# A transposed copy of x1 by DMA instead of TensorE, o_rec in PSUM, and a new order on GpSimd and VectorE

## What is computed

```python
# 1. causal attention over x with one more key and value made from cond (16 heads of 16)
q, k, v = split(x @ c_attn_w + c_attn_b); k = concat(k_img, k); v = concat(v_img, v)
a = softmax(where(causal, q @ k.T / 4, -10000) + mask) @ v @ c_proj_w + c_proj_b
# 2. linear attention over a, a residual and a layer norm
q2, k2, v2 = relu(a @ Wq.T + bq), relu(a @ Wk.T + bk), a @ Wv.T + bv
y = (q2 @ (k2.T @ v2)) / max(q2 @ sum(k2), 1e-6) + a
x1 = x + layernorm(y) * gamma + beta
# 3. an LSTM over the 64 rows of each sequence as time steps (batch 64), then an FP4 FFN
for t in range(64): gates = x1[:, t] @ Wx + h @ Wh + b; c, h = cell(gates, c)
out = x1 + (silu(fp4(h) @ fp4(w_gate).T) * (fp4(h) @ fp4(w_up).T)) quantized again @ fp4(w_down).T
```

## Time and profile before

| | us |
|---|---|
| median of 3 runs | 1044.33 |
| lowest, highest | 1040.74, 1045.4 |
| profiled execution | 1042.76 |
| its span, first to last instruction | 1040.8 |
| busy in the span: TensorE, VectorE, ACT, GpSimd | 892.0, 885.0, 500.4, 343.1 |
| mean granted clock of TensorE | 0.95 of full speed |

### The profile page before, as it was taken

The page is one execution under the profiler, slowest core; times in us unless marked ns, Lnnn a source line. Parts: engine busy times, 40 slices in busy tenths (PEclk is TensorE's granted clock), DMA queues, the critical chain, the costliest instruction groups (busy, mean ns, idle before and its releaser), DMA issues. The chain is left out here.

```text
span 1040.8 us, 27556 instructions
## 1 busy us (share of the span) xinstructions
PE 892.0 (86%) x9862; PEld 595.3 (57%) x9862; DVE 885.0 (85%) x2157; ACT 500.4 (48%) x1177; POOL 343.1 (33%) x436
## 2 busy tenths in 40 slices
PE   3477887988888888888987799999999999999984
PEld 2255555666666666666655456656565566656553
DVE  5489889799999999999985488888888888888884
ACT  2356446466667666766664333334433333434431
POOL 0126446455555555555563011111111111111111
PEclk9589789799999999999998999999999999999997
DMA  4500000101110111011100000000000000000001
GB/s 109 190 13 22 27 19 18 35 19 34 33 33 17 33 33 33 18 32 33 34 22 16 11 7 16 22 21 21 21 21 21 21 17 16 20 21 21 21 21 26
DMA packets 37143, 30.37 MB, mean 29 GB/s; under 512 B 12081, under 2 KB 35953, under 8 KB 37076
## 3 DMA queue, kind: packets, MB, share of 16 engines
q1 hardware_dynamic: 37076, 29.42, 10.0%
HBM read 20.87 MB, written 8.54 MB: 28 GB/s over the span
## 5 line engine op out<-in xcount | busy, mean ns | idle before, releaser
L663 POOL TENSOR_TENSOR ffn_room<-h_value,h_scale 128x704 f32<-128x704 f32 x32 | 44.3, 1386 | 292.7 <-DVE h_value L171 292.7
L711 PE MATMUL bank<-gu,xqT 128*128 128x512 f16 (+1 forms) x576 | 130.1, 366 | 0.7 <-DVE xqT L1542 0.7
L886 PE MATMUL bank<-wh,h 128*64 128x512 f16 x768 | 100.3, 385 | 3.5 <-ACT h L1157 2.1
L875 PE MATMUL bank<-wx,x1T 128*64 128x512 f16 x768 | 93.7, 379 | 0.9 <-DVE x1T L440 0.9
L611 POOL TENSOR_TENSOR p<-prob,p 128x520 f16<-128x520 f32 x64 | 79.1, 1236 | 43.6 <-ACT p L1065 43.6
L987 PE MATMUL bank<-dn,hqT 128*128 128x256 f16 x576 | 70.7, 279 | 19.6 <-DVE hqT L1527 19.6
L1147 ACT ACTIVATE sig<-bank 128x256 f32<-128x256 f32 x64 | 24.6, 385 | 127.3 <-PE bank L886 126.7
L875 PEld LDWEIGHTS bank<-wx,x1T 128*64 128x64 f16 x768 | 78.6, 201 | 11.4 <-DVE x1T L440 1.2
L711 PEld LDWEIGHTS bank<-gu,xqT 128*128 128x128 f16 x576 | 54.2, 99 | 53.9 <-issue 11.3
L776 PE MATMUL bank<-ident,p 128*65 128x128 f16 x1024 | 78.8, 228 | 1.4 <-POOL p L611 0.8
L604 POOL TENSOR_TENSOR prob<-prob,row_max 128x520 f32<-128x520 f32 x64 | 68.2, 1066 | 31.0 <-DVE row_max L1325 31.0
(11 more groups left out here) (201 smaller groups left out, 2192.2 us busy)
## 6 DMA issues: line engine op xcount, KB each, us to landing
x_in<-in_x SPq DMA_DIRECT2D x32, 128.0 KB, 2.2
x_res<-in_x SPq DMA_DIRECT2D x32, 128.0 KB, 2.1
x_rows<-x_rows_sb SPq DMA_DIRECT2D x32, 128.0 KB
ffn_room<-x_rows SPq DMA_DIRECT2D x64, 64.0 KB, 2.2
out<-ffn_room SPq DMA_DIRECT2D x64, 64.0 KB, 2.0
mask_in<-in_mask_Bx1x1xS_ff SPq DMA_DIRECT2D x64, 16.0 KB, 2.4
x1T<-in_L_cond_Wx SPq DMA_DIRECT2D x1, 1024.0 KB, 6.2
x1T<-in_L_cond_Wh SPq DMA_DIRECT2D x1, 1024.0 KB, 8.2
```

What stands on the lines that cost most here:

```text
L663: pool.tensor_tensor(blocks(hq, FF), blocks(fp4_h.value, FF), spread(fp4_h.scale, FF), ALU.mult).then_inc(s["hq_ready"], 1)
L711: last = pe.matmul(dst, lhs(a, c), rhs(b, c), start=first and c == 0 and a == b, stop=c == C - 1 and (a, b) == parts3[-1], skip_group_chec ...
L875: last = pe.matmul(bank[e][B * h:B * h + B, :], x1T16[m][:, c, :, at], half_cols(wx16, a, c, h), start=False, stop=True, skip_group_check= ...
L886: last = pe.matmul(bank[e][B * h:B * h + B, :], h16[:, m, c, :], half_cols(wh16, a, c, h), start=False, stop=True, skip_group_check=True)
```

## The change

- x1 isn't transposed by TensorE any more. ACT casts `x1_rows` to the high half of a new SBUF buffer `x1_split`, GpSimd subtracts for the low half, and SP issues one transposing DMA per tile from `x1_split` into `x1T_all`, which holds both parts in one tensor. ACT's cast waits for the DMA of the tile before; the LSTM waits for the DMAs of all tiles.
- `o_rec` lies in PSUM (`bank[5]`) instead of SBUF, and the two plain copies of the qk split read PSUM instead of SBUF.
- On GpSimd, the softmax work of t2 and the image keys come ahead of zg and x1 of t5; the new subtraction stands between `res_rows` and the variance.
- On VectorE, z is made one step later (as t5), behind the head mask, and `add_mask` stands behind the low part of v.
- On SP, x is asked for one tile ahead of t1.

```diff
--- before.py
+++ after.py
@@ -225,9 +225,10 @@
     eps_ln = sb("eps_ln", [P, 1])
-    x1T16 = [sb(f"x1T16_{i}", [P, C, B, S], F16) for i in range(2)]
-    x1T_room = [t[:, :, :, :].rearrange("p c b s -> p (c b s)").bitcast(F32) for t in x1T16]
+    x1T_all = sb("x1T16", [P, 2, C, B, S], F16)
+    x1T16 = [x1T_all[:, i] for i in range(2)]
+    x1T_room = [t.rearrange("p c b s -> p (c b s)").bitcast(F32) for t in x1T16]
     bias_cols = sb("bias_cols", [P, BIAS_C])
@@ -265,7 +266,7 @@
     pT = sb("pT", [KEYS, 2, 2, 4, P], F16)
-    o_rec = sb("o_rec", [P, H])
+    o_rec = bank[5][:, 512 - H:512]
     o_sum = sb("o_sum", [P, H, HD])
@@ -288,6 +289,7 @@
     x1_rows = sb("x1_rows_sb", [P, D])
+    x1_split = sb("x1_split", [P, 2, D], F16)
     sig = sb("sig", [P, 6 * B])
@@ -322,7 +324,7 @@
         kv_ps kv_masked ctx_ps den_ready den_inv ctx_div resid stats_ready mean_ready var_ready
-        rstd_ready z_ready zg_ready xb_ready x1_ready x1_ps x1T_hi x1T_lo x1_stored
+        rstd_ready z_ready zg_ready xb_ready x1_ready x1_hi x1_lo x1T_in x1_stored
         gates_ps sig_if sig_o tanh_g i_g cell_ready tanh_c h_ready h_hi h_lo
@@ -430,16 +432,6 @@
     parts3 = ((0, 0), (0, 1), (1, 0))
-    def x1_part(eng, t, part):
-        src = bank[2][:, D:2 * D].rearrange("p (c n) -> p c n", c=C)
-        dst = [x1T16[i][:, :, bass.ds(t.number() * 2, 2), :].rearrange("p c b s -> p c (b s)") for i in range(part + 1)]
-        if part == 0:
-            last = eng.copy(dst[0], src)
-        else:
-            last = eng.tensor_tensor(dst[1], src, dst[0], ALU.subtract)
-        last.then_inc(s["x1T_lo" if part else "x1T_hi"], 1)
     def mask_count(t):
@@ -520,9 +512,11 @@
                 q = t1.parity
-                after(sp, s["xT_ps"], t1.count(back=2))
-                if t1.loop is not None or t1.b > 0:
-                    sp.dma_start(x_in[:, q, :], x_tiles[t1.number()]).then_inc(x_loaded[q], 16)
+                if t1.loop is not None or t1.b < NT - 1:
+                    ahead = Tile(t1.loop, t1.b + 1)
+                    after(sp, s["xT_ps"], ahead.count(back=2))
+                    sp.dma_start(x_in[:, 1 - q, :], x_tiles[ahead.number()]).then_inc(x_loaded[1 - q], 16)
                 after(sp, s["mask_ready"], t1.count(back=2))
@@ -544,6 +538,9 @@
                 sp.dma_start(x1_tiles[t5.number()], x1_rows[:, :]).then_inc(s["x1_stored"], 16)
+                sp.wait_ge(s["x1_lo"], t5.count())
+                sp.dma_start_transpose(x1T_all[:, :, :, bass.ds(t5.number() * 2, 2), :].rearrange("p i c b s -> p (i c) (b s)"),
+                                       x1_split[:, :, :].rearrange("p i d -> p (i d)")).then_inc(s["x1T_in"], 16)
         pipeline(sp, 5, step, first=10)
@@ -612,24 +609,23 @@
             t1, t2, _, t4, t5 = tiles
+            if t2:
+                shift(t2, 1)
+                probs_lo(t2, 0)
+                probs_lo(t2, 1)
+            if t1:
+                after(pool, s["scores_ps"], t1.count(2, 2, back=1))
+                pool.tensor_copy(kT[:, :, :, S:KEYS].rearrange("p h b o -> p h (b o)"),
+                                 kimgT[:, :, bass.ds(t1.number() * 2, 2)]).then_inc(s["kimg_in"], 1)
             if t5:
...
                 pool.wait_ge(s["xb_ready"], t5.count())
-                after(pool, s["x1_ps"], t5.count(back=1))
                 after(pool, s["x1_stored"], t5.count(per=16, nth=16, back=1))
                 pool.tensor_tensor(x1_rows[:, :], zg_rows[:, :], xb_rows[:, :], ALU.add).then_inc(s["x1_ready"], 1)
-            if t2:
-                shift(t2, 1)
-                probs_lo(t2, 0)
-                probs_lo(t2, 1)
-            if t1:
-                after(pool, s["scores_ps"], t1.count(2, 2, back=1))
-                pool.tensor_copy(kT[:, :, :, S:KEYS].rearrange("p h b o -> p h (b o)"),
-                                 kimgT[:, :, bass.ds(t1.number() * 2, 2)]).then_inc(s["kimg_in"], 1)
             if t4:
@@ -645,6 +641,11 @@
                 pool.tensor_tensor(res_rows[:, :], ctx_rows[:, :], y_rows[:, :], ALU.add).then_inc(s["resid"], 1)
+            if t5:
+                pool.wait_ge(s["x1_hi"], t5.count())
+                pool.tensor_tensor(x1_split[:, 1, :], x1_rows[:, :], x1_split[:, 0, :], ALU.subtract).then_inc(s["x1_lo"], 1)
+            if t4:
                 pool.wait_ge(s["mean_ready"], t4.count())
@@ -728,7 +729,6 @@
                 pe.wait_ge(s["setup_done"], 1)
-            after(pe, s["x1T_lo"], t.count(back=5))
             lhs = lambda a, c: xT16[:, a, P * c:P * c + P]
@@ -933,9 +933,6 @@
                     lstm_state(Tile(None, 0), 0)
-                if not t1:
-                    pe.wait_ge(s["x1T_lo"], t5.count(back=1))
-                rows_transpose(t5, bank[2][:, D:2 * D], x1_rows, "x1_ready", "x1_ps")
             if t3:
@@ -989,7 +986,7 @@
             last.then_inc(s["down_ps"], 1)
-        pe.wait_ge(s["x1T_lo"], NT)
+        pe.wait_ge(s["x1T_in"], 16 * NT)
         pe.wait_ge(s["ffn_done"], len(ffn_plan))
@@ -1123,6 +1120,11 @@
             chore(t1, 1)
+            if t5:
+                act.wait_ge(s["x1_ready"], t5.count())
+                after(act, s["x1T_in"], t5.count(per=16, nth=16, back=1))
+                act.copy(x1_split[:, 0, :], x1_rows[:, :]).then_inc(s["x1_hi"], 1)
             if t3:
@@ -1132,8 +1134,6 @@
                     ffn_hi(t5, "end")
-                act.wait_ge(s["x1_ps"], t5.count())
-                x1_part(act, t5, 0)
         pipeline(act, 5, step, first=10)
@@ -1349,11 +1349,6 @@
                 last.then_inc(s["o_added"], 1)
-            if t1:
-                dve.wait_ge(mask_loaded[t1.parity], mask_count(t1))
-                after(dve, s["masked"], t1.count(2, 2, back=1))
-                dve.scalar_tensor_tensor(out=add_mask[:, 0:S], in0=mask_in[:, t1.parity, :], scalar=SCORE,
-                                         in1=causal[:, 0:S], op0=ALU.mult, op1=ALU.add).then_inc(s["mask_ready"], 1)
             if t3:
@@ -1374,7 +1369,7 @@
                     dve.tensor_tensor(qk16[:, r, lo_at, :], heads[:, r, :], qk16[:, r, 0, :], ALU.subtract)
-                    dve.tensor_copy(qk16[:, r, hi_at, :], qk16[:, r, 0, :]).then_inc(s["qk_split"], 1)
+                    dve.tensor_copy(qk16[:, r, hi_at, :], heads[:, r, :]).then_inc(s["qk_split"], 1)
             if t4:
@@ -1385,6 +1380,11 @@
                 ffn_lo(t4, "outer")
+            if t5:
+                dve.wait_ge(s["rstd_ready"], t5.count())
+                after(dve, s["zg_ready"], t5.count(back=1))
+                dve.tensor_scalar(z_rows[:, :], res_rows[:, :], mean_var[:, 0:1], rstd[:, 0:1], ALU.subtract, ALU.mult)\
+                    .then_inc(s["z_ready"], 1)
             if t1:
@@ -1392,6 +1392,11 @@
                 last.then_inc(s["v_lo"], 1)
+            if t1:
+                dve.wait_ge(mask_loaded[t1.parity], mask_count(t1))
+                after(dve, s["masked"], t1.count(2, 2, back=1))
+                dve.scalar_tensor_tensor(out=add_mask[:, 0:S], in0=mask_in[:, t1.parity, :], scalar=SCORE,
+                                         in1=causal[:, 0:S], op0=ALU.mult, op1=ALU.add).then_inc(s["mask_ready"], 1)
             if t4:
@@ -1437,18 +1442,11 @@
                 masked(t1, 1)
-            if t4:
-                dve.wait_ge(s["rstd_ready"], t4.count())
-                after(dve, s["zg_ready"], t4.count(back=1))
-                dve.tensor_scalar(z_rows[:, :], res_rows[:, :], mean_var[:, 0:1], rstd[:, 0:1], ALU.subtract, ALU.mult)\
-                    .then_inc(s["z_ready"], 1)
             if t1:
...
                     ffn_lo(t5, "end")
-                dve.wait_ge(s["x1T_hi"], t5.count())
-                x1_part(dve, t5, 1)
             chore(t1, 1)
...
```

More of the change, by code:

```diff
@@ L632, in step @@
                                  kimgT[:, :, bass.ds(t1.number() * 2, 2)]).then_inc(s["kimg_in"], 1)
+            if t5:
+                pool.wait_ge(s["z_ready"], t5.count())
+                pool.tensor_tensor(zg_rows[:, :], z_rows[:, :], gamma_sb[:, :], ALU.mult).then_inc(s["zg_ready"], 1)
+                pool.wait_ge(s["zg_ready"], t5.count())
+                pool.wait_ge(s["xb_ready"], t5.count())
+                after(pool, s["x1_stored"], t5.count(per=16, nth=16, back=1))
+                pool.tensor_tensor(x1_rows[:, :], zg_rows[:, :], xb_rows[:, :], ALU.add).then_inc(s["x1_ready"], 1)
             if t4:
```

8 lines of the change are left out of this document (1 added, 7 removed).

## The result

| | before | after |
|---|---|---|
| median of 4 runs in turn on one chip, us | 1042.53 (1040.31 to 1045.4) | 1015.76 (1015.53 to 1018.06) |
| ratio, 95% interval | | 0.9747 [0.9714, 0.9779] |
| span of the profiled execution, us | 1040.8 | 1013.9 |
| cast of tile 0 to cast of tile 9 (9 early steps) | 171.0 | 152.7 |
| cast 9 to cast 31 (22 steps) | 326.2 | 315.1 |

The change takes 2.5% off. The forecast was 13 us, the runs show 27, a value of rival C. The last four rows of the table come from the timeline of ACT's x casts and of TensorE's first product on x1T, in the two traces. They say where it went: 18.3 us in the early steps, 11.1 in the steady ones, and 2.4 given back behind the last cast. They stand on one execution of each kernel.

A forecast was written before the change was run, and what follows sets the result against it. The attention step was taken as a ring through TensorE, ACT and VectorE, not VectorE's busy time alone. Steady steps -6, early steps -13, end +6 summed to -13 us from 1042.76: forecast 1030 us, range 1012 to 1047.

The forecast's parts named there:

- rival C: More gain than forecast: the clock holds in the early steps and little contention returns, 1008 to 1018 us; chance 0.13.
- front, cast of x to qkv's start: Steady step ahead of qkv: earlier low part of xT removes only TensorE's mean wait of 0.40 us; -0.37 a step.
- qk copies, split to head mask: Steady step behind VectorE's wait for ACT: copies reading PSUM shorten the 1.75 us split; -0.40 us, ends 0 and -0.5.
- z and mask add: Steady step: z moved behind the head mask adds 0.33 us, the mask add moved behind v adds 0.20.
- The early steps: Nine steps before the steady 22, VectorE bounding their front too: -13 us together, ends -5 and -22.
- the clock term: Early steps: shorter TensorE waits for the split should keep 2.4 GHz in some steps; -3 us, ends 0 and -8.
- the work term: Early steps: VectorE work and contention removed, less what returns behind the split; -10 us.
- The end: Behind the last x1: cast, subtraction, DMA issue and landing, late last res, slower TensorE clock; +6 us, ends +3 and +12.
- A: Rival: transposing DMA holds SP from 7 us of issue, masks come late; about 1110 us at 10 us issue; chance 0.12.
- B: Rival: z or mask add meets GpSimd's ops in its new place, 0.5 to 0.7 us a step; 1040 to 1046; chance 0.2.
- D: Rival: VectorE's busy time shrinks but nothing is gained, the ring being tighter than read; 1038 to 1042 us; chance 0.07.
- the ring: Attention step as closed chain of waits: VectorE work ahead of the qk split counts only where delaying xT, behind it fully.

The follow-up runs named there:

- e1_orec: Kernel before with only the reciprocals of the softmax sums (o_rec) put in PSUM: ratio 0.9863, median 1026.1 us.
- e3_pool: Kernel before with only GpSimd's zg and x1 moved behind its softmax work: ratio 0.9848, median 1023.4 us.
- e2_qk: Kernel before with only the two qk copies reading PSUM: ratio 0.9798, median 1019.6 us.
- e6_idle: Kernel after with z and mask add moved between o_rows and the qk split, GpSimd's zg and x1 between its two low parts: ratio 0.9598 to before, 997.9 us.
- e9_delay3: Kernel after with three small unused VectorE reductions ahead of xT's low part: single run, 1021.3 us, steady step 14.49 us.
- e12_warm2: Kernel before with many unused TensorE products filling its waits in steps 4, 5, 6 and 8, no VectorE work removed: ratio 0.9889, 1029.6 us.
- e7_fill12: Kernel after with 12 useless small stores issued on SP behind each transposing DMA: single run, 1019.2 us, steady step 14.35 us.

## Why the prediction came out as it did

**What bounded the kernel: right.** e1_orec and e3_pool each shortened VectorE's work ahead of the split by some 1 us without moving the steady step, e2_qk's saving behind it came through whole, and e6_idle gained by moving work from the one part to the other.

**The steady step: -0.24 to -0.27 forecast, -0.58 measured.** In offsets from ACT's cast of x (means of the 21 steady steps of each trace):

| term | forecast | measured |
|---|---|---|
| front, cast of x to qkv's start | -0.37 | -0.57 (1.85 to 1.28) |
| qk copies, split to head mask | -0.40 | -0.41 |
| z and mask add | +0.33 +0.20 | +0.45 |
| the rest | 0 (-0.03) | -0.05 |

The term that was mis-sized is the first: "TensorE turns only its wait, 0.40 us on the mean, into time". The mechanism held. The size was read from the idle time that the rows give ahead of qkv's first matmul, and the spacing of starts shows that this understates a wait by 0.17 us in the kernel before and by 0.19 in e9_delay3; with 0.17 added, the mean wait of 0.40 is the 0.57 measured. That (0.20) and the cheaper z and mask (0.08) make 0.28 of the 0.31 a step that the forecast lacks, and all of it together 5 us of the 14 that were missing. The 22 steps give 11.1 us and not 22 x 0.58, since the one from cast 9 to cast 10 grew by 1.0, from 14.8 to 15.8.

**The early steps: -13 forecast, -18.3 measured.** All of it is in steps 4, 5, 6 and 8, which went from 87.1 to 68.2 us (-18.9). The prediction had "-3, ends 0 and -8" for the clock and -10 for the work. e12_warm2, with full clock and all of the old work, has 77.0: the low clock cost 10.1 us there, and 8.8 lie between e12_warm2 and after. The kernel after is not at full clock, though. It went from 0.80 to 0.95 from 95 to 195 us, three quarters of the way to 1.00, so an estimate from these two rows is that it got back 7 to 8 of the 10.1, and that its work and new order are worth 11. So the step of the prediction that failed here is the clock term, "-3, ends 0 and -8": it measured 7 to 10 by the two ways of counting, while the work term of -10 was near. The split is by one order of the edits: e1_orec and e3_pool each gained 13 us in these four steps with 1 us less to do in each, at a clock of 0.91 and 0.90, so a little work taken off can bring the clock along. Why just some of the waits lead to 1.2 GHz was not resolved beyond the rows above.

**The end: +6 forecast, +2.4 measured.** The chain behind the last x1 in after:
```profile
543.29 0.72 POOL L628 TENSOR_TENSOR x_rows_sb<-zg_rows,xb_rows 128x256 f32<-128x256 f32 x1
544.04 0.40 ACT L1127 CAST x_split<-x_rows_sb 128x256 f16<-128x256 f32 x1 [4.77 <-POOL x_rows_sb L628]
...
544.52 0.67 POOL L647 TENSOR_TENSOR x_split<-x_rows_sb,x_split 128x256 f16<-128x256 f32 x1 [0.51 <-ACT x_split L1127]
...
545.22 1.20 SPq L542 DMA_TRANSPOSE x1T<-x_split  x1
...
547.68 1.57 PE L875 MATMUL bank<-wx,x1T 128*64 128x512 f16 x6 [3.14 <-DMA x1T<-x_split]
```
From x1's end at 544.01 to the product it is 3.67 us, where before it was 1.46: +2.2, under the +3 to +5 forecast, as the issue and the landing overlap (2.4 together; the sum counted them one after the other). The mechanism was right. The clock cost came as said, 1.5 us: this stretch is granted 0.51, and six products take 1.57 us where twelve took 1.58. What was left out is the clock ahead of the last x1. The last x1 is ready 51.1 us after the last cast where it was 52.4, at a clock of 0.95 where it was 0.87. By the three rows of the old program above, a clock of 0.95 alone would have brought it to about 49.5 (an estimate by straight line between 50.3 and 47.7). So at a like clock the new order makes this part some 1.6 us longer, within the "+1 to +2" for the last res behind z, x1 and xb, and the clock gave back about 3. This term is an estimate and no run isolates it; the prediction had put it at nothing.

**The rivals.** A: the ring of SP is there, at the price that the prediction worked out, and the transposing DMA's 1.21 us is a fifth of what it would take (1.2 + the 4.9 that e7_fill12 added with next to no wait). B: z at 0.42 and the mask add at 0.21 on the mean of 32, so that a meeting in the new places costs next to nothing. This hangs on an order that the rows show and that was forecast: GpSimd has done its low part and waits for z. The rival's premise that every product with two SBUF operands met something holds for the lines and not for each instance, as the mask add's least time of 0.207 shows. C: this is what came, with its chance of 0.13. Most of the early steps' excess is the clock, as it says; the front term of the steady step, which brought about as much, is not in it. D: falls with e1_orec and e2_qk.

**What was to show it.** Right as written: VectorE near 80% with 2.4 us of waiting for ACT, the copies at 0.41, o_rows at 0.29, z at 0.40, no wait for xT, early steps under 19 us. Wrong: steady steps of 14.25, not 14.55, and the first LSTM product 3.7 us after x1, not 4 to 6.

In sum: the 27 us of span are the forecast 13, 5 more in the steady steps, 5 more in the early ones, 4 less lost behind the last cast. The account of what bounds the kernel held. What failed is the price of TensorE's clock, -3 in the early steps where 7 to 10 were due and nothing ahead of the last x1 where about 3 were, and the price of TensorE's wait for xT, 0.37 a step where 0.57 was due.

## What to carry to other kernels

Find the ring first and then ask in which part of it an edit's work stands; in the steady steps a VectorE at 97.5% gave nothing for 1 us ahead of the split and all for 0.38 behind it, and the free part is the place for what can move (e6_idle: another 1.5% on top). Price a TensorE wait by the start-to-start distance against the same group without the wait, not by the idle time in its row. Where the granted clock is below 1.00 and the rows show matmuls at half speed behind waits, price the clock as its own term with its own experiment: small products in the wait are a cheap one. And before a few us between two traces are put down to an edit, compare the granted clock of the two stretches.
